# A macaron block on one core: the first tile, the two changes of stage and the last store put in another order

## The chip, the cores and the metric

The kernel runs on one core of one Trainium2 chip. The metric is the time of one execution on the device in microseconds (us); less is better. PE is TensorE, DVE VectorE, ACT ScalarE, POOL GpSimd, and SP the engine whose queue issues the DMAs.

## What is computed

x has 8 batches of 1024 rows of 128 numbers, all f32. Three residual steps follow one another, each on a layer norm of x:

```python
x = x + 0.5 * ffn(layernorm(x))
x = x + attn(layernorm(x))          # rotated q and k, causal softmax, one head of width 128
x = x + 0.5 * ffn(layernorm(x))     # the same weights

# ffn: 16 experts of width 64, 4 of them weighted per row, and one shared expert
scores = sigmoid(x @ gate_w.T)
w = scores of the 4 largest of (scores + gate_b), divided by their sum, times 2.5
y = sum_e w[e] * ((silu(x @ g_e.T) * (x @ u_e.T)) @ w2_e.T)  +  shared expert
```

## The kernel before

**Stages.** The first ffn runs over 16 tiles of 512 rows (T = 0 to 15), then attention over 8 batches, then the second ffn over 16 tiles (T = 16 to 31). All of x stays in SBUF, and the result is stored tile by tile in the second ffn. Every engine has its program written out by hand, with semaphores between them.

**One tile of the ffn.** All experts are computed, two at a time: `PAIRS` = 8 units of two experts, and unit 8 is the shared one (`UNITS` = 9). Each f32 product is made of three matmuls on a high and a low half of its factors (`mm3`). For a unit j, PE writes the gate and the up product to PSUM (`ffn_up`), ACT takes silu of the gate in place (`ffn_silu`), DVE multiplies by the row's weights of the two experts (`ffn_weighted`) and by the up product (`ffn_h`), ACT rounds this h to its high half (`ffn_h_hi`), POOL subtracts to get the low half (`low_half`, `h_lo_done`), and PE multiplies by w2 (`ffn_down`), three units later (`LAG`). After the last unit ACT copies the sum (`ffn_yT`), PE transposes it (`ffn_y`), and DVE adds it to x (`residual`).

**Routing.** During tile T the weights of tile T+1 are made: PE `ffn_logits`, then a chain of small DVE steps (`ffn_logit0` to `ffn_comb`, counted by `route_step`, 13 steps) with one ACT step in it (`ffn_gsilu`: score = silu(logit) / logit). PE transposes them (`ffn_combT`), ACT copies, and SP writes them to HBM and loads them back spread over the partitions (`comb_rows`, ten loads of up to 256 KB), which `ffn_weighted` reads.

**The first tile.** There is no time for that round trip, so for its first four units DVE copies the weights 64-fold into `spread`, PE transposes them (`comb_spread`), and ACT copies the result to `comb_s`. Only units 4 to 7 use the loads. The weights w13 come in two loads (`early`: 4 blocks, then 13) and are split by ACT and POOL. `warm` issues matmuls on zeros: 20, 5, 10 and 2 of them.

**From the first ffn to attention.** In tile 15 the projections of batch 0 (`qkv`), the rotation (`rope_cos` and `rope_add` on DVE, `rope_sin` on POOL) and the transposes (`qkT`) are woven in, by unit, by the tables `FIRST_STEPS`, `SIN_STEPS`, `COS_STEPS` and `ADD_STEPS`; ACT's copies come one unit later, at the end of the unit's work. After the tile PE does the first scores, `qkT` 2 and 3, the transposes of xn of batch 1 (`xnT` 0 and 1), and then `ffn_y(15)`.

**From attention to the second ffn.** In the last batch, `ffn_prep(i)` on each engine prepares tile 16 and the norm of tile 17 at row block i. Exp and Silu are in different tables of ACT.

## Time and profile before

| what | value |
|---|---|
| time, median of 3 runs | 886.3 us (885.8 to 886.94) |
| the profiled execution: its time | 890.32 us |
| its span in the profile | 888.5 us |
| PE busy | 866.8 us (98%) |
| DVE, ACT, POOL busy | 77%, 68%, 64% |
| mean granted clock of PE | 0.99 of full |

The span is from the first to the last instruction or transfer that the profile shows; 1.8 us lie around it. A view by stretches gives for each the busy time of the engines and the granted clock (1.00 is 2.4 GHz, 0.50 is 1.2 GHz). A line of the time line has start, duration, engine, line of the kernel, operation and tiles, and in brackets for how long the engine had been idle and who released it. A name of a tile can be that of the memory that it shares: `prob` stands for the weighted gate, `probT` for h, `cos` for `spread`, `sin` for `comb_s`, `qkv_both` for the loaded weights.

### The profile page before, as it was taken

The numbers are of one execution on the slowest core, as the hardware profiler recorded it, in microseconds if no ns is written. First come the engines' busy times: TensorE is split into PE (matmuls) and PEld (weight loads), VectorE is DVE, ScalarE is ACT, GpSimd is POOL, SyncE is SP. The second block draws the span as 40 slices with busy tenths as digits, with TensorE's granted clock in tenths as the row PEclk, the third lists the DMA queues.
The fourth block names the chain that finished last, engine by engine and source line by source line (L and its number), as shares of the span: only waits on it lengthen the run. The fifth ranks groups of instructions, "written<-read, shape, count | busy, mean of one in ns | idle before, by whom it ended". The sixth has DMA issues, their size and how long they took to land.

```text
span 888.5 us, 18704 instructions
## 1 busy us (share of the span) xinstructions
PE 866.8 (98%) x4634; PEld 732.4 (82%) x4634; DVE 687.3 (77%) x2123; ACT 603.3 (68%) x1255; POOL 568.3 (64%) x605
## 2 busy tenths in 40 slices
PE   8999999999999997999999999999999999999997
PEld 7778888888888875999999998788888888888885
DVE  6888888888888887565555656688888888888884
ACT  4666666666666675677777777776666666666664
POOL 5666666666667674866668763166666666666664
PEclk9999999999999999899999999999999999999998
DMA  3486444555554430000000000334455554444552
GB/s 119 134 236 144 108 108 109 122 132 134 136 122 96 97 97 1 1 1 1 1 0 0 0 0 0 97 97 110 120 132 137 132 124 108 108 109 122 137 133 63
DMA packets 58212, 80.61 MB, mean 91 GB/s; under 512 B 6464, under 2 KB 25152, under 8 KB 57920
## 3 DMA queue, kind: packets, MB, share of 16 engines
q1 hardware_dynamic: 58176, 80.19, 36.6%
q8 instruction: 15, 0.25, 0.1%
q14 instruction: 21, 0.17, 0.1%
HBM read 74.92 MB, written 5.24 MB: 90 GB/s over the span
## 4 chain that ended last, share of the span: by engine, by line
PE 56%; ACT 3%; DVE 2%; issue 1%; POOL 0%; ACTq 0%; DVEq 0%
PE bank L1189 49%; PE bank L1441 3%; PE bank L1405 2%; PE bank L1257 1%; PE bank L1236 1%; PE bank L1394 1%; ACT prob L651 1%; DVE xl L1069 1%; ACT probT L492 0%; ACT qkv_both L492 0%; ACT xh L492 0%; DVE probT L838 0%; ACT h_h L492 0%; DVE prob L829 0%; PE bank L1250 0%
## 5 line engine op out<-in xcount | busy, mean ns | idle before, releaser
L370 POOL TENSOR_TENSOR h_l<-probT,h_h 128x512 fp32r<-128x512 f32 x256 | 330.9, 1293 | 215.6 <-ACT h_h L492 215.4
L492 ACT ACTIVATE h_h<-probT 128x512 fp32r<-128x512 f32 (+1 forms) x288 | 180.2, 626 | 72.2 <-DVE probT L838 70.8
L1189 PE MATMUL bank<-xh,w_h 128*128 128x512 f32 x544 | 223.2, 410 | 0.3
L521 ACT ACTIVATE bank<-bank 128x512 f32<-128x512 f32 x256 | 148.6, 581 | 103.7 <-PE bank L1189 99.6
L1189 PE MATMUL bank<-xh,w_l 128*128 128x512 f32 x544 | 214.2, 394 | 0.0
L829 DVE TENSOR_TENSOR prob<-bank,qkT 128x512 f32<-128x512 f32 x252 | 173.6, 689 | 52.3 <-ACT bank L521 38.6
L1189 PE MATMUL bank<-xl,w_h 128*128 128x512 f32 x544 | 212.7, 391 | 0.0
L838 DVE TENSOR_TENSOR probT<-prob,bank 128x512 f32<-128x512 f32 x256 | 174.5, 681 | 11.5 <-DVE biased L772 5.0
L1189 PEld LDWEIGHTS bank<-xh,w_h 128*128 128x128 f32 x544 | 102.4, 188 | 23.4 <-DVE probT L838 3.5
L1189 PEld LDWEIGHTS bank<-xh,w_l 128*128 128x128 f32 x544 | 102.1, 188 | 23.7
L1189 PEld LDWEIGHTS bank<-xl,w_h 128*128 128x128 f32 x544 | 102.6, 189 | 19.2
L1189 PE MATMUL bank<-h_h,w_h 128*128 128x512 f32 x288 | 116.9, 406 | 1.5 <-POOL h_l L370 1.1
L1189 PE MATMUL bank<-h_h,w_l 128*128 128x512 f32 x288 | 113.6, 395 | 0.0
L1189 PE MATMUL bank<-h_l,w_h 128*128 128x512 f32 x256 | 101.3, 396 | 0.0
L492 ACT ACTIVATE probT<-bank 128x512 f32<-128x512 f32 (+2 forms) x128 | 64.8, 515 | 49.4 <-PE bank L1441 46.8
L1189 PE MATMUL bank<-qkv_both,probT 128*128 128x128 f32 x576 | 76.0, 277 | 2.4 <-ACT probT L492 1.3
L1189 PEld LDWEIGHTS bank<-qkv_both,probT 128*128 128x128 f32 x576 | 71.7, 192 | 4.8 <-issue 1.8
L466 POOL TENSOR_TENSOR rope_c<-qkv_both,cos 128x256 f32<-128x256 f32 x56 | 41.0, 733 | 48.2 <-ACT qkv_both L492 48.2
L499 ACT ACTIVATE xn<-X,neg_shift,rstd 128x128 f32 (+1 forms) x128 | 61.2, 485 | 9.9 <-POOL neg_shift L379 9.9
L1189 PEld LDWEIGHTS bank<-h_h,w_h 128*128 128x128 f32 x288 | 54.2, 188 | 15.0 <-POOL h_l L370 1.8
L1189 PE MATMUL bank<-qkT 128*128 128x512 f32 (+3 forms) x288 | 65.7, 355 | 0.0
L1189 PEld LDWEIGHTS bank<-h_h,w_l 128*128 128x128 f32 x288 | 54.2, 188 | 10.8
(103 smaller groups left out, 1396.2 us busy)
## 6 DMA issues: line engine op xcount, KB each, us to landing
...
```

Of the source, the lines that this page charges most:

```text
L370: nc.gpsimd.tensor_tensor(lo, f, hi.bitcast(F32), ALU.subtract).then_inc(done, 1)
L466: nc.gpsimd.tensor_tensor(rope_c[s][:], qkv[p][:, n, 0:2 * D].rearrange("p (w d) -> p w d", w=2), cos[:, n, :, :], ALU.mult).then_inc(rope ...
L492: return nc.scalar.activation(dst, src, ACT.Copy)
L499: ins = nc.scalar.activation(xn[:, n, :], X[:, bass.ds(NB * Tx + n, 1), :].rearrange("p a d -> p (a d)"), ACT.Identity, bias=neg_shift[:, ...
L521: nc.scalar.activation(bank[:, G_BANK[g], :], bank[:, G_BANK[g], :], ACT.Silu).then_inc(silu_done, 1)
L651: nc.scalar.activation(prob[s][:, 0:w], bank[:, 2 * s:2 * s + 2, :].rearrange("p a c -> p (a c)")[:, 0:w], ACT.Exp, bias=negmax[s][:], sca ...
L829: nc.vector.tensor_tensor(weighted[j % 2], bank[:, G_BANK[(q + j) % 2], :], comb_s[:, j, :] if spread_out else comb_b[q][:, j, :], ALU.mul ...
L838: nc.vector.tensor_tensor(h[g], weighted[j % 2], bank[:, U_BANK[j % 2], :], ALU.mult).then_inc(h_done, 1)
L1069: nc.vector.tensor_tensor(xl_half[n][:], bank[:, m, :], xh_half[n][:].bitcast(F32), ALU.subtract).then_inc(a_xl_done, 1)
L1189: return nc.tensor.matmul(dst, lhsT, rhs, start=start, stop=stop)
L1405: ins = nc.tensor.transpose(bank[:, m, c:c + P], rot[(2 * n + a) % ROPE_BUFS][:, w, :], ident[:])
L1441: ins = nc.tensor.transpose(bank[:, probT_bank(i, c, last), a * P:(a + 1) * P], prob[s][:, k0:k0 + P], ident[:])
```

## The change

It touches four places.

- **First tile.** w13 comes in three loads (4, 4 and 9 blocks). The silu of units 0 to 3 goes to SBUF (`silu_s`), and the spread weights are read where PE put them, in PSUM. The spread of units 0 and 1 is made by four DVE operations straight from `wsel` and `rsum`, before `ffn_comb`, that of 2 and 3 by two ACT copies. PE runs four gate and three up products ahead of the spread, then two more gates and two ups, with three banks for up (`START_U_BANK`). `ffn_xl(0, 0)` goes ahead of the statistics of tile 1. `warm` issues 16 and 5.
- **From the first ffn to attention.** ACT makes its copies for attention at the head of a unit. POOL makes the shift of batch 1 behind its last low half of the tile, and `rope_sin` and `rope_cos` of blocks 6 and 7 come earlier. ACT asks for its Exp table on a dummy before the `qkT` 2 copy. PE does `ffn_y(15)` ahead of the xn transposes of batch 1, and DVE `residual` ahead of `qkT` 3.
- **From attention to the second ffn.** The score of tile 16 is 1 / (1 + exp(-logit)), by Exp. ACT normalizes tile 17 at i = 6 instead of i = 7, ahead of its copies of the last `probT`, and asks for the Silu table at i = 7.
- **End.** In tile 31 DVE makes the low halves of units 7 and 8, PE orders its last products by what is there first, and copy, transposes, residual and store go in two halves.

Semaphores, tensors and calls that only follow from these are left out below, and some indentation. Constants:

```diff
-SPREAD_BANK = 4, 6
+SPREAD_BANK = 4, 5, 4, 4
...
-SIN_STEPS = [[], [0], [], [1], [2], [3], [4], [5], [6]]
-COS_STEPS = [[], [0], [], [1, 2], [], [3, 4], [], [5], [6]]
...
+      ("qkT", 0): 5, ("qkv", 5): 7, ("qkv", 6): 5, ("qkT", 1): 7, ("qkv", 7): 5, ("qkT", 2): 5, ("qkT", 3): 7}
+SIN_STEPS = [[], [0], [], [1], [2], [3], [4], [5, 6], [7]]
+COS_STEPS = [[], [0], [], [1, 2], [], [3, 4], [], [5, 6], []]
...
+ON_DVE = 2
+AHEAD = 3
+WARM = 16, 5
...
-early = slice(0, 2 * EARLY), slice(2 * EARLY, 2 * UNITS - 1)
+early = slice(0, 4), slice(4, 8), slice(8, 2 * UNITS - 1)
```
SP:

```diff
+load(w13_f[:, early[1], :], w13T[:, early[1], :], w13_loaded[1])
 load(X[:, NB:2 * NB, :], x_v[:, NB:2 * NB, :], x_loaded[1])
-load(w13_f[:, early[1], :], w13T[:, early[1], :], w13_loaded[1])
+load(w13_f[:, early[2], :], w13T[:, early[2], :], w13_loaded[2])
 load(w2_f, w2T, w2_loaded)
...
-        store(TILES - 1)
+        for a in range(2):
+            sp.wait_ge(x_done, 2 * TILES + a)
+            sp.dma_start(out_v[:, end_blocks(a), :], X[:, end_blocks(a), :]).then_inc(stored, 16)
```
POOL (the first piece is in the loop over units):

```diff
+        if last and first_batch is None and j >= PAIRS - 1:
...
-                pool.wait_ge(a_neg_shift_done, 2)
-            elif first_batch == 1:
-                pool.wait_ge(rope_s_done, QB - 1)
+            if first_batch == 1:
+                pool.wait_ge(rope_s_done, QB)
...
-        elif j == PAIRS - 1 and first_batch == 0:
+        elif j == PAIRS and first_batch == 0:
+            pool.wait_ge(h_lo_done, UNITS * (T + 1))
...
         low_half(w13_l[:, early[0], :], w13_f[:, early[0], :], w13_h[:, early[0], :], w13_split[0])
+        pool.wait_ge(w13_hi[1], 1)
+        low_half(w13_l[:, early[1], :], w13_f[:, early[1], :], w13_h[:, early[1], :], w13_split[1])
         pool.wait_ge(neg_shift_done, 1)
...
         ffn_tile(TILES - 1, 1, True, 1)
-        pool.wait_ge(h_lo_done, UNITS * TILES)
-        rope_sin(0, 0, QB - 1)
```
ACT:

```diff
-    if j < PAIRS:
+    if isinstance(T, int) and T == 0 and j < SPREAD:
+        nc.scalar.activation(silu_s[:, j, :], bank[:, G_BANK[g], :], ACT.Silu).then_inc(silu_done, 1)
...
 def comb_spread(j):
-    act.wait_ge(spread_ready, j + 1)
-    copy(comb_s[:, j, :], bank[:, SPREAD_BANK[j % 2], :]).then_inc(spread_done, 1)
+    act.wait_ge(route_step, ROUTE)
+    copy(spread[:, j, :, :].rearrange("p n (a r) -> p n a r", a=2),
+         comb[:, 2 * j:2 * j + 2, :].rearrange("p a (n r) -> p n a r", r=1
+                                               ).to_broadcast([P, NB, 2, INTER])).then_inc(spread_copied, 1)
 def ffn_tile(T, Tx, q, first, last, first_batch=None, start=False):
     for j in range(UNITS):
+        if first_batch == 1 and j >= 1:
+            for item in FIRST_STEPS[j - 1]:
...
         if j == 0 and not last and not start:
             ffn_xh(T + 1, 1 - q)
         if j == (7 if start else 6) and not last:
             ffn_combT(T + 1, 1 - q)
-        if not start or j >= 1:
+        if not start or j >= SPREAD:
...
             for n in XN_STEPS[j]:
                 attn_xn(1, n)
-            for item in FIRST_STEPS[j - 1] if j else []:
...
         act.wait_ge(w13_loaded[1], 16)
         copy(w13_h[:, early[1], :], w13_f[:, early[1], :]).then_inc(w13_hi[1], 1)
+        ffn_xh(base, 0)
         ffn_gsilu(base)
+        ffn_silu(base, 0, 0)
+        act.wait_ge(w13_loaded[2], 16)
+        copy(w13_h[:, early[2], :], w13_f[:, early[2], :]).then_inc(w13_hi[2], 1)
+        ffn_silu(base, 0, 1)
+        ffn_silu(base, 0, 2)
         for n in range(NB):
             ffn_xn(base + 1, 1, n)
-        ffn_silu(base, 0, 0)
         act.wait_ge(w2_loaded, 16)
         copy(w2_h[:], w2_f).then_inc(w2_hi, 1)
-        comb_spread(0)
         ffn_combT(base, 0)
-        comb_spread(1)
+        comb_spread(2)
         ffn_xh(1, 1)
-        comb_spread(2)
+        ffn_silu(base, 0, 3)
+        ffn_h_hi(base, 0, 0)
         comb_spread(3)
     ffn_tile(base, 0, 0, True, False, None, start)
...
+    if start:
+        attn_item(("qkv", 7), 0, 0, True)
     ffn_h_hi(T, 1, UNITS - 1)
     if start:
-        attn_item(("qkv", 7), 0, 0, True)
+        nc.scalar.activation(table[:, 0:1], X[:, B * QB, 0:1], ACT.Exp)
         attn_item(("qkT", 2), 0, 0, True)
         attn_exp(0, 0, 0)
-    ffn_yT(T, 1)
+        ffn_yT(T, 1)
+    else:
+        ffn_end(T)
+def ffn_end(T):
+    act.wait_ge(down_done, UNITS * (T + 1))
+    act.wait_ge(y_ready, T)
+    for a in range(2):
+        cols = slice(2 * P * a, 2 * P * (a + 1))
+        copy(yT[:, cols], bank[:, Y_BANK[1], cols]).then_inc(yT_half, 1)
 def attn_item(item, b, p, prologue=False):
...
-        ffn_gsilu(T)
+        ffn_exp_neg(T)
     elif i == 6:
         ffn_combT(T, 0)
-    elif i == 7:
         for n in range(NB):
             ffn_xn(T + 1, 1, n)
+    elif i == 7:
+        nc.scalar.activation(table[:, 1:2], X[:, B * QB, 0:1], ACT.Silu)
```
DVE:

```diff
+def ffn_denominator(T):
+    dve.wait_ge(gsilu_done, T + 1)
+    nc.vector.tensor_scalar_add(logit[:], gsilu, 1.0).then_inc(route_step, 3)
+def ffn_sigmoid(T):
+    dve.wait_ge(route_step, ROUTE * T + 4)
+    nc.vector.reciprocal(score, logit[:]).then_inc(route_step, 1)
...
+    if isinstance(T, int) and T == 0 and j < SPREAD:
+        dve.wait_ge(spread_ready, j + 1)
+        nc.vector.tensor_tensor(weighted[j % 2], bank[:, SPREAD_BANK[j], :], silu_s[:, j, :],
+                                ALU.mult).then_inc(weighted_done, 1)
...
+        low_half(h_h[k][INTER:P, :], h[g][0:INTER, :], h_h[k][0:INTER, :], h_lo_end)
+def ffn_end(T):
+    for a in range(2):
+        dve.wait_ge(y_half, a + 1)
+        xt = X[:, end_blocks(a), :]
+        nc.vector.scalar_tensor_tensor(xt, bank[:, END_BANK[a], 0:2 * P].rearrange("p (n d) -> p n d", d=D), 0.5, xt,
+                                       ALU.mult, ALU.add).then_inc(x_done, 1)
...
     if start:
-        ffn_weighted(T, q, 0)
-        ffn_h(T, q, 0)
+        for j in range(2):
+            ffn_weighted(T, q, j)
+            ffn_h(T, q, j)
         ffn_xl(N, 1 - q)
         dve.wait_ge(x_loaded[2], 16)
         for n in range(NB):
             ffn_stats(L, Lx, n)
-        ffn_weighted(T, q, 1)
...
         ffn_stats_wait(L)
         ffn_mv(L)
...
+        ffn_h(T, q, 2)
         ffn_var(L)
         ffn_logit0(N)
-        ffn_weighted(T, q, 2)
         ffn_away0(N)
         ffn_logit(N)
-        ffn_h(T, q, 2)
+        ffn_weighted(T, q, 3)
         ffn_recip(N)
-        ffn_weighted(T, q, 3)
+        ffn_h(T, q, 3)
         ffn_score(N)
         ffn_bias(N)
         ffn_biased(N)
...
         if first_batch == 1:
             attn_start(PAIRS)
+        else:
+            ffn_h_lo(T, q, PAIRS - 1)
...
+    ffn_xl(0, 0)
     dve.wait_ge(x_loaded[1], 16)
...
-    ffn_xl(0, 0)
     ffn_logit0(0)
...
     ffn_top4(0)
-    ffn_weights(0)
+    ffn_wsel(0)
+    ffn_wsum(0)
+    ffn_rsum(0)
+    comb_spread(0)
+    comb_spread(1)
+    ffn_comb(0)
+def comb_spread(j):
+    dve.wait_ge(route_step, ROUTE - 1)
+    for a in range(2):
+        e = 2 * j + a
+        ins = nc.vector.scalar_tensor_tensor(spread[:, j, :, a * INTER:(a + 1) * INTER],
+                                             wsel[:, :, e:e + 1].to_broadcast([P, NB, INTER]), ROUTE_SCALE,
+                                             rsum[:].rearrange("p (n r) -> p n r", r=1).to_broadcast([P, NB, INTER]),
+                                             ALU.mult, ALU.mult)
+    ins.then_inc(spread_set, 1)
...
         ffn_start()
-        dve.wait_ge(route_step, ROUTE)
-        for j in range(SPREAD):
-            nc.vector.tensor_copy(spread[:, j, :, :].rearrange("p n (a r) -> p n a r", a=2),
...
     if start:
+        rope_add(0, QB - 2)
         rope_cos(0, 0, QB - 1)
-        rope_add(0, QB - 2)
+        rope_add(0, QB - 1)
         dve.wait_ge(scores_ready, 1)
         attn_max(0, 0)
-        rope_add(0, QB - 1)
         attn_item(("qkT", 2), 0, 0, True)
+        residual(base + TILES - 1, TILES - 1)
         attn_item(("qkT", 3), 0, 0, True)
-    residual(base + TILES - 1, TILES - 1)
+    else:
+        ffn_end(base + TILES - 1)
...
-        ffn_recip(T)
     elif i == 5:
-        ffn_score(T)
+        ffn_denominator(T)
+        ffn_sigmoid(T)
         ffn_bias(T)
```
PE:

```diff
-    if j >= 2:
-        pe.wait_ge(spread_done, j - 1)
-    pe.wait_ge(spread_set, j + 1)
+    if j < ON_DVE:
+        pe.wait_ge(spread_set, j + 1)
+    else:
+        pe.wait_ge(spread_copied, j - ON_DVE + 1)
+        pe.wait_ge(weighted_done, 1 if j == 2 else j)
     for n in range(NB):
-        ins = nc.tensor.transpose(bank[:, SPREAD_BANK[j % 2], n * P:(n + 1) * P], spread[:, j, n, :], ident[:])
+        ins = nc.tensor.transpose(bank[:, SPREAD_BANK[j], n * P:(n + 1) * P], spread[:, j, n, :], ident[:])
     ins.then_inc(spread_ready, 1)
+def start_gate(j):
+    if 2 <= j < SPREAD + 2:
+        pe.wait_ge(silu_done, j - 1)
+    elif j >= SPREAD + 2:
+        pe.wait_ge(weighted_done, j - 1)
+    mm3(bank[:, G_BANK[j % 2], :], w13_h[:, 2 * j, :], w13_l[:, 2 * j, :], xh[0][:], xl[0][:]).then_inc(gate_ready, 1)
+def start_u(j):
+    if j >= AHEAD:
+        pe.wait_ge(h_done, j - AHEAD + 1)
+    mm3(bank[:, START_U_BANK[j % 3], :], w13_h[:, 2 * j + 1, :], w13_l[:, 2 * j + 1, :],
+        xh[0][:], xl[0][:]).then_inc(up_ready, 1)
...
     pe.wait_ge(w13_split[0], 1)
-    for j in range(EARLY):
-        ffn_up(0, 0, j, None)
-    warm(WARM[2])
+    for j in range(AHEAD):
+        if j == 2:
+            pe.wait_ge(w13_split[1], 1)
+        start_gate(j)
+        start_u(j)
+    start_gate(AHEAD)
     comb_spread(0)
+    comb_spread(1)
     ffn_combT(0)
-    comb_spread(1)
-    warm(WARM[3])
     ffn_xnT(1)
     comb_spread(2)
+    start_u(3)
+    pe.wait_ge(w13_split[2], 1)
+    start_gate(4)
+    start_u(4)
+    start_gate(5)
+    ffn_logits(1, 1)
     comb_spread(3)
+    pe.wait_ge(w2_split, 1)
+    pe.wait_ge(weighted_done, 2)
+    ffn_down(0, 0, 0)
+    for j in range(5, UNITS):
+        if j >= 6:
+            start_gate(j)
+        if j < PAIRS:
+            start_u(j)
+        if j == 6:
+            ffn_combT(1)
+        ffn_down(0, 0, j - AHEAD - 1)
+    ffn_down(0, 0, UNITS - LAG - 1)
...
         attn_item(("qkT", 3), 0, 0, True)
+    ffn_y(T)
     if start:
-        for item in STEP_ITEMS[0][:2]:
-            attn_item(item, 1, 1)
...
+        attn_item(("xnT", 0), 1, 1)
+def ffn_end(T):
+    Y = bank[:, Y_BANK[1], :]
+    a, b = PAIRS - 1, PAIRS
+    pe.wait_ge(h_hi_done, UNITS * T + a + 1)
+    mm(Y, w2_h[:, a, :], h_h[a % 3][:], False, False)
+    mm(Y, w2_l[:, a, :], h_h[a % 3][:], False, False)
+    pe.wait_ge(h_hi_done, UNITS * T + b + 1)
+    mm(Y, w2_l[0:INTER, b, :], h_h[b % 3][0:INTER, :], False, False)
+    pe.wait_ge(h_lo_end, 1)
+    mm(Y, w2_h[:, a, :], h_l[a % 3][:], False, False)
+    pe.wait_ge(h_lo_end, 2)
+    mm(Y, w2_h[:, b, :], h_h[b % 3][:], False, True).then_inc(down_done, 2)
+    pe.wait_ge(x_done, T)
+    for n in range(NB):
+        c = n % 2
+        if c == 0:
+            pe.wait_ge(yT_half, n // 2 + 1)
+        ins = nc.tensor.transpose(bank[:, END_BANK[n // 2], c * P:(c + 1) * P], yT[:, n * P:(n + 1) * P], ident[:])
+        if c == 1:
+            ins.then_inc(y_half, 1)
...
             attn_scores(b, p, i + 1)
         elif not last:
             attn_scores(b + 1, 1 - p, 0)
-        before, after = ([], []) if last else ([], STEP_ITEMS[0][2:]) if first and i == 0 else step_items(i)
+        before, after = ([], []) if last else step_items(i)
```
## Rows read from the trace of the kernel before

**Rows 1.** The page: busy time and share of the engines, first line.

```profile
PE 866.8 (98%) x4634; PEld 732.4 (82%) x4634; DVE 687.3 (77%) x2123; ACT 603.3 (68%) x1255; POOL 568.3 (64%) x605
```

**Rows 2.** The chain that ended last: start us, us, what (second ffn).

```profile
597.14 1.38 PE bank L1189 x6
...
616.84 1.38 PE bank L1189 x6
```

**Rows 3.** Time line, first tile, all engines but SP, 8 to 39 us.

```profile
8.64 1.28 PE L1189 MATMUL bank<-X 128*128 128x128 f32 x10
...
11.37 0.30 DVE L750 TENSOR_REDUCE bank<-bank 128x64 f32<-128x128 f32 x1 [1.21 <-PE bank L1189]
...
11.54 1.60 ACT L492 ACTIVATE w_h<-qkv_both 128x1664 fp32r<-128x1664 f32 x1 [2.11 <-DMA qkv_both<-in_w13T]
...
13.21 6.58 POOL L370 TENSOR_TENSOR w_l<-qkv_both,w_h 128x1664 fp32r<-128x1664 f32 x2 [2.77 <-ACT w_h L492]
13.34 0.23 DVE L768 TENSOR_TENSOR bank<-bank,rlogit 128x64 f32<-128x64 f32 x1 [0.57 <-ACT bank L510]
...
15.98 0.28 DVE L816 SCALAR_TENSOR_TENSOR comb<-bank,rsum 128x64 f32<-128x64 f32 x1
16.29 4.46 DVE L1026 COPY cos<-comb 128x512 f32<-128x512 f32 x4
...
20.67 0.68 DVE L829 TENSOR_TENSOR prob<-bank,sin 128x512 f32<-128x512 f32 x1
...
23.59 0.69 DVE L743 TENSOR_TENSOR xl<-bank,xh 128x512 fp32r<-128x512 f32 x1 [1.52 <-ACT xh L492]
...
34.62 0.33 PE L1250 MATMUL bank<-ident,comb 128*128 128x128 f32 x1
...
38.98 0.60 PE L1236 MATMUL bank<-ident,xn 128*128 128x128 f32 x4
```

**Rows 4.** Line 1026, DVE's four copies: shortest, median and longest in ns.

```profile
L1026 DVE COPY cos<-comb x4: 415/706/2866, 16.3 to 20.3; 128x512 f32<-128x512 f32 x4
```

**Rows 5.** By stretches: PE, PEld, DVE, ACT, POOL busy, granted clock, DMA share, GB/s.

```profile
22.00:23.00 1.00, 1.00 (x7) 1.00 (x6) 0.07 (x1) 0.04 (x1) 0.00 (x0) 0.50 0.78 213
...
359.00:361.00 2.00, 2.00 (x8) 1.87 (x7) 0.32 (x2) 1.45 (x4) 1.59 (x3) 0.50 0.00 0
```

**Rows 6.** Time line, from tile 15 to batch 0, 343 to 356 us.

```profile
343.26 1.24 DVE L1052 TENSOR_TENSOR rope_c<-qkv_both,cos 128x256 f32<-128x256 f32 x1
...
347.47 1.28 ACT L651 ACT_TABLE_LOAD   x1
...
350.97 1.71 PE L1394 MATMUL bank<-ident,xn 128*128 128x128 f32 x8 [1.97 <-DVE qkT L1074]
...
355.35 0.66 PE L1189 MATMUL bank<-wqkv_h,xh 128*128 128x384 f32 x1 [0.56 <-DVE xl L1069]
```

**Rows 7.** Time line, last batch to tile 16, 559 to 570 us.

```profile
559.76 0.98 PE L1441 MATMUL bank<-ident,prob 128*128 128x128 f32 x7 [0.66 <-ACT prob L651]
...
564.32 2.02 PE L1189 MATMUL bank<-qkv_both,probT 128*128 128x128 f32 x16 [0.34 <-ACT probT L492]
564.54 1.64 ACT L499 ACTIVATE xn<-X,neg_shift,rstd 128x128 f32<-128x128 f32 x4
...
569.51 0.69 DVE L829 TENSOR_TENSOR prob<-bank,qkT 128x512 f32<-128x512 f32 x1 [0.48 <-ACT bank L521]
```

**Rows 8.** Time line, the end, from 879 us.

```profile
879.37 0.69 DVE L841 TENSOR_TENSOR probT<-prob,bank 64x512 f32<-64x512 f32 x1 [0.28 <-ACT prob L524]
...
882.53 0.50 PE L1189 MATMUL bank<-h_h,w_h 128*128 128x512 f32 x1 [0.39 <-POOL h_h L370]
...
883.30 0.60 ACT L492 ACTIVATE probT<-bank 128x512 f32<-128x512 f32 x1 [2.58 <-PE bank L1189]
...
885.11 0.69 DVE L865 SCALAR_TENSOR_TENSOR X<-bank,X 128x512 f32<-128x512 f32 x1 [5.05 <-PE bank L1257]
885.83 0.40 SPq L321 DMA_DIRECT2D out_x<-X  x1
```

103 lines of the change are left out of this document (56 added, 47 removed).

## The prediction

> **What bounds the kernel now.** I read the page first: PE is busy for 98% of the span [rows 1], so nothing is won by making another engine faster in the steady part. The chain that ended last says the same: in the second ffn the same piece of PE work comes back after 19.70 us for every tile (616.84 less 597.14), and nothing but PE stands between [rows 2]. What can be won lies where PE waits or does work that counts for nothing, and the change touches just the places where that happens. So I read the time line of each, and ask one question: by how much does PE come earlier to the first piece of work behind which it never waits again? What is won before such a point is kept to the end, since the loops behind it are PE's.
>
> **First tile.** PE starts tile 1 (xn transposes) at 38.98, behind the transpose of tile 1's weights at 34.62, which follows at once on DVE's `ffn_comb(1)` [rows 3]. DVE is what sets this tile. Its main work starts at 20.67, with `ffn_weighted(0)`. The reader is to see what stands ahead of it: four copies that take 4.46 us [rows 3].
>
> Step 1, the logits. Four of 20 fill matmuls go; a fill record takes 0.13 us (1.28 / 10), two records make one, so PE would be free up to 1.0 us earlier, but then waits for xn. Against this, the split of xn is now in front of the statistics, which delays the first step of the route (11.37). I take -0.4 (0 to -0.7).
>
> Step 2, the score. It starts at 13.34 after 0.57 of idling for ACT's silu, which stood behind the 1.60 us copy of the 13 weight blocks (from 11.54) [rows 3]. That copy now comes behind gsilu. So -0.5 more: the route is 0.9 earlier, and DVE is where `ffn_comb` began (15.98) at 15.1.
>
> Step 3, the spread. DVE now makes four operations of 256 elements for the first two units. No row has one of this form. The nearest below is `ffn_comb` itself, 64 elements, 0.28; above, a DVE operation of 512 elements, 0.69 [rows 3]. Between, with their overlap, I take 0.37 each: 1.5 in all (1.0 to 2.8). With `ffn_comb` that puts `ffn_weighted(0)` at 16.9, 3.8 before the 20.67 of now. PE's transposes of the first spread run under the second one.
>
> Why the copies took 4.46: of the four, the shortest took 0.415 us and the longest 2.87 [rows 4], while POOL ran its low halves, 6.58 us from 13.21 on [rows 3]. One copy sat until POOL was done. The Trainium skill, page "SBUF — State Buffer", section "SBUF: two separate sides", has the rule: DVE operations of certain kinds and GpSimd take a shared port pair as an exclusive lock, for the whole instruction. The long copy agrees. By it the new operations, with one input in PSUM and one in SBUF, wait for nobody, and my 1.5 stands. If they were held as the copy was, it would be the case "held" below.
>
> Step 4, the DVE work up to `ffn_comb(1)`. Now 20.67 to 34.6, 13.9 us. 1.52 of it is a wait for ACT's xh [rows 3]; it goes, since PE and ACT are now ahead with the transposes of tile 1. What is left, 12.4, is the same list of operations without a gap; I take 12.5 (12 to 13.5). So `ffn_comb(1)` ends at 29.4, 5.2 earlier.
>
> Step 5, PE. It has to be ready by then. It has 11 groups of three 512-column matmuls (0.69 each: six take 1.38 [rows 2]) done before unit 5, where it had 4. Behind the transpose of the weights it now has one `ffn_down` more, 0.7: tile 1 starts 4.5 earlier. PE idles about 2 us before that, where gate 6 waits for `ffn_weighted(4)`. The clock was 0.50 at 22 to 23 us, behind a PE that had waited between the spreads [rows 5]. Such a fall again costs 0 to 1.3; I take 0.3. ACT's spread copies, POOL's splits and the extra SP issue (0.40, as the one in [rows 8]) lie beside all this: ACT wants the second w13 load only after the first, and DVE wants the X load later than now, since the split of xn is in front of it. POOL's last split ends about 20, and its first low half is wanted by `ffn_h(2)` at 22. First tile: **-4.2** (-2.5 to -5.2).
>
> **Tile 15 to batch 0.** The end point is the first qkv product of batch 1 at 355.35, behind which the batch runs on PE [rows 6]. In tile 15 ACT's copies at the head of a unit take away some PE waits, but DVE sets the pace there and gives back most. What stays: the rotation `cos` of block 6 begins at 343.26, behind ACT's copy [rows 6]; now it is ahead of `ffn_h(8)`. That makes `qkT` 1 come 1.9 earlier, and the maximum of row block 0 1.4 earlier. The table load, 1.28, [rows 6] goes from between `qkT` 2 and exp to a place where ACT waits for PE anyway: exp 2.5 earlier, `ffn_yT` 2.3. Then `ffn_y(15)` no longer stands behind `qkT` 3, the wait of 1.97 and the eight xn transposes of 1.71 [rows 6]: the residual is 5 earlier. Behind it come now the low half of `qkT` 3 and the maximum, 1.1 together. Sum at the qkv product: **-4.7** (-3.0 to -7.2).
>
> The lower bound: DVE has now cos 5, cos 6 and the add of 4 before `ffn_h(8)`, and each cos can be 1.24 long. The upper bound is the clock. At 359 to 361 it is 0.50 with PE busy all the time [rows 5], after the 1.97 wait. If PE does not fall, work of some 5 us at half speed takes half: -2.5 more.
>
> On the table load page and trace differ. The row has 1.28 from the end of the copy before to exp's start, with 0.01 between. The Trainium skill, page "ScalarE: Activation LUTs", section "What ACT_TABLE_LOAD costs", gives 2.66 us for a switch, a drain of 1.38 included. By the page this term would be -6.1; the measurement decides.
>
> **Last batch to tile 16.** Two table loads go from ACT's path and PE loses its wait of 0.66 before the transposes at 559.76 [rows 7]. But the four normalizations, 1.64, which ran beside PE's product at 564.32 [rows 7], now stand in front of the copy that this product waits for. With 0.7 won before, the weights are copied at about 562.5, the normalizations end at 564.1 and the copy at 564.7: the product starts 0.4 later than now. What sets the end is `ffn_weighted` of tile 16 at 569.51, 0.48 after DVE was ready, since silu had its table load [rows 7]. That load is hidden now, so DVE starts when ready: 0.4 later and 0.5 earlier, **0.0** (-0.4 to +1.8, with a clock fall in the new wait of 1.6).
>
> **End.** PE's last group waits until 882.53 for POOL, and ACT's copy is at 883.30 [rows 8]. POOL's two low halves lie ahead of it one behind the other, 1.3 each. DVE takes 0.69 for one of 512 elements, has nothing else behind 879.37 + 0.69, and ACT's high halves come a little before each: both are made by 881.4, and one matmul is left: copy at 881.9, not 883.30. Half copies, transposes and residuals overlap: now 883.30 to 885.80, 2.5; in halves I take 1.85 (1.5 to 2.5): -0.65. A second store issue (0.40 [rows 8]) is under the second half. **-2.1** (-1.4 to -2.5).
>
> **Sum.** -4.2 - 4.7 + 0.0 - 2.1 = -11.0. The profiled execution took 890.32 (888.5 span and 1.8 around it): 879.3 by its own time. The median of the runs is 886.3, 4.0 lower, and no term scales with that: **875.3**.
>
> **Rivals.**
> - *PE keeps its clock at the start of batch 0*: 2.5 more, 872.8. For it: the gaps of about 2 us become several of at most 0.8. Against it: they are many, and PE is busy little more than half of the time there.
> - *Held or late*: the first tile gives little. If the new spread operations are held until POOL's 9-block split ends (16.4), 1.5 is lost; with the clock at half behind the 2 us wait of step 5, 1.0 more; or the new wait of the last batch takes 1.5: 878.3. The page's lock speaks against the first part, rows 5 for the second.
> - *It does not do what it says*: tile 1 has its own gate, `ffn_weighted(0)` of tile 1, which waits for the round trip of `comb_rows`, and the residual of tile 15 moves but not the products behind it. Only the end is left: 884.2. Against it: that trip starts with the transpose of the weights (34.62), 4 earlier too.
> - *Slower*: the fills that go (4 of 20, and all 12 behind the routing) held PE's clock up. One place: from 9 to 34 us. PE's real work there is 23 groups of 0.69 and about 3 us of transposes and logits, 19 us at full clock; at half all along it would take 19 more, 894. It decides from 11 us on. Against it: PE now has products where the fills were, and falls last a few us in the rows. [...]
>
> **How the numbers follow.** Forecast (873.8 to 877.2) 0.50, clock kept 0.18, held or late 0.25, not done 0.04, slower 0.02, none of these 0.01. The measurement tells apart about 0.2%, 1.8 us. Faster by more than that: 0.50 + 0.18 + 0.25 + 0.04 = 0.97, less 0.01 for sums of bad ends, 0.96; same 0.02; slower 0.02. The range takes in the first three with their own widths: 871.5 to 879.5.
>
> **What the profile after would show.** Step 2: score at about 12.4. Step 3: `ffn_weighted(0)` near 16.9, and no DVE operation longer than 0.5 before it. Step 5: tile 1's xn transposes at 34.5. Batch 0: Exp table load ahead of the `qkT` 2 copy, first qkv product of batch 1 about 8.9 earlier than 355.35. Tile 16: its first weighted operation unchanged against that shift. End: last matmul to last residual under 2 us. I am wrong if DVE has waits above 1 us between 17 and 29 us, if PE's clock is 0.50 for more than 4 us in the first tile, or if tiles in the loops take other than 19.70.

## The result and the profile after

Timed beside each other, the changed kernel takes 875.93 us (median of 4, 875.33 to 876.56) and the kernel before 886.62 us (median of 4, 885.8 to 887.35). The ratio is 0.988, with a 95% interval of 0.9863 to 0.9897: 10.7 us less. The profiled execution of the changed kernel has a span of 874.6 us; that of before had 888.5, so the two traces differ by 13.9, 3.2 more than the medians. A second profile of before, below, shows where most of the 3.2 come from.

The page's first line of engines, after (compare [rows 1]):

```profile
PE 858.0 (98%) x4602; PEld 725.2 (83%) x4602; DVE 684.9 (78%) x2124; ACT 601.5 (69%) x1255; POOL 566.0 (65%) x604
```

The chain that ended last, in the second ffn (start, us, what; compare [rows 2]):

```profile
592.75 0.44 PE bank L1355 x4
...
612.49 0.44 PE bank L1355 x4
```

PE is still all there is in a tile, but a tile takes 19.74 (612.49 less 592.75), not 19.70.

The time line of the first tile (compare [rows 3, 4]):

```profile
12.54 0.23 DVE L818 TENSOR_TENSOR bank<-bank,rlogit 128x64 f32<-128x64 f32 x1
...
15.19 1.42 DVE L1089 SCALAR_TENSOR_TENSOR cos<-bank,rsum 128x256 f32<-128x256 f32 x4
16.52 0.27 DVE L866 SCALAR_TENSOR_TENSOR comb<-bank,rsum 128x64 f32<-128x64 f32 x1
16.76 0.69 DVE L874 TENSOR_TENSOR prob<-bank,sin 128x512 f32<-128x512 f32 x1
...
27.12 0.54 PE L1271 MATMUL bank<-xh,w_h 128*128 128x512 f32 x1 [1.91 <-DVE prob L881]
...
28.89 0.28 DVE L866 SCALAR_TENSOR_TENSOR comb<-bank,rsum 128x64 f32<-128x64 f32 x1
...
35.15 0.60 PE L1355 MATMUL bank<-ident,xn 128*128 128x128 f32 x4
```

The four copies of 4.46 us have become four operations of 1.42 in all, and `ffn_weighted(0)` starts at 16.76, not 20.67. DVE has no wait from there to 31.8. PE's longest is the 1.91 us before gate 6, the gate product of unit 6; the next is 0.55. What comes of it stands in the view by stretches (PE, PEld, DVE, ACT, POOL busy, granted clock, DMA share, GB/s; compare [rows 5]):

```profile
27.00:28.00 1.00, 0.88 (x3) 0.74 (x4) 1.00 (x10) 0.00 (x0) 0.29 (x1) 0.72 1.09 376
28.00:29.00 1.00, 1.00 (x4) 0.81 (x3) 0.90 (x5) 0.72 (x2) 0.01 (x1) 0.50 1.00 371
...
352.00:354.00 2.00, 2.00 (x16) 1.87 (x15) 1.00 (x5) 1.45 (x4) 1.87 (x4) 1.00 0.00 0
```

The clock is at half (1.2 GHz) to about 31 us, 3.4 us in all. At the start of batch 0, where before it was at half, it stays full (1.00 in the last row). The time line there (compare [rows 6]):

```profile
338.81 1.28 ACT L656 ACT_TABLE_LOAD   x1
...
339.70 1.45 POOL L385 TENSOR_TENSOR h_h<-probT,h_h 64x512 fp32r<-64x512 f32 x1
339.94 1.49 DVE L1136 TENSOR_TENSOR rope_c<-qkv_both,cos 128x256 f32<-128x256 f32 x1
...
341.81 0.29 DVE L1165 CUSTOM_DVE_ANT_0 bank<-bank,mask 128x128 f32<-128x128 f32 x1
342.19 0.37 ACT L692 ACTIVATE prob<-bank,negmax 128x128 f32<-128x128 f32 x1 [1.11 <-DVE negmax L1165]
343.89 0.69 DVE L935 SCALAR_TENSOR_TENSOR X<-bank,X 128x512 f32<-128x512 f32 x1 [1.19 <-PE bank L1376]
...
346.26 0.41 PE L1271 MATMUL bank<-wqkv_h,xh 128*128 128x384 f32 x1 [0.38 <-DVE xl L1153]
```

The table is loaded while ACT has nothing else; the first qkv product of batch 1 starts at 346.26, not 355.35. The last batch (compare [rows 7]):

```profile
550.60 1.64 ACT L515 ACTIVATE xn<-X,neg_shift,rstd 128x128 f32<-128x128 f32 x4
552.14 1.06 ACT L508 ACTIVATE probT<-bank 128x512 f32<-128x512 f32 x2
...
552.87 2.02 PE L1271 MATMUL bank<-qkv_both,probT 128*128 128x128 f32 x16 [1.60 <-ACT probT L508]
...
557.49 0.69 DVE L881 TENSOR_TENSOR prob<-bank,qkT 128x512 f32<-128x512 f32 x1
```

The normalizations now stand in front of the copies, and PE waits 1.60. The end (compare [rows 8]):

```profile
868.28 0.68 DVE L763 TENSOR_TENSOR h_l<-probT,h_h 128x512 fp32r<-128x512 f32 x1
...
869.08 0.49 PE L1271 MATMUL bank<-h_h,w_l 64*128 64x512 f32 x1 [0.20 <-ACT h_h L508]
...
870.40 0.66 ACT L508 ACTIVATE probT<-bank 128x256 f32<-128x256 f32 x2 [1.37 <-PE bank L1271]
...
871.37 0.75 DVE L911 SCALAR_TENSOR_TENSOR X<-bank,X 128x256 f32<-128x256 f32 x2 [1.63 <-PE bank L1486]
871.83 0.91 SPq L365 DMA_DIRECT2D out_x<-X  x2
```

### The profile page after: what moved, and what is told of

Read it like the earlier page. It is cut to its first block, busy times and chain, and to the rows that moved or that the text cites. A ratio compares the mean times of both kernels' runs of the same rounds, so it can differ in the third digit from the quotient of the medians.

```text
span 874.6 us, 18644 instructions
## 1 busy us (share of the span) xinstructions
PE 858.0 (98%) x4602; PEld 725.2 (83%) x4602; DVE 684.9 (78%) x2124; ACT 601.5 (69%) x1255; POOL 566.0 (65%) x604
## 4 chain that ended last, share of the span: by engine, by line
PE 55%; DVE 3%; ACT 2%; issue 1%; POOL 0%; ACTq 0%; DVEq 0%
PE bank L1271 48%; PE bank L1580 3%; PE bank L1544 1%; PE bank L1376 1%; PE bank L1355 1%; DVE xl L1153 1%; PE bank L1533 0%; ACT xh L508 0%; ACT qkv_both L508 0%; ACT prob L692 0%; ACT xn L515 0%; ACT probT L508 0%; DVE prob L881 0%; DVE rope_c L1136 0%; PE bank L1369 0%
## 5 line engine op out<-in xcount | busy, mean ns | idle before, releaser
L543 ACT ACTIVATE bank<-bank 128x512 f32<-128x512 f32 x252 | 146.3, 581 | 103.4 <-PE bank L1271 98.9
```

The source lines that it names most:

```text
L543: nc.scalar.activation(bank[:, G_BANK[g], :], bank[:, G_BANK[g], :], ACT.Silu).then_inc(silu_done, 1)
```

## The experiments

The changed kernel was timed twice: medians of 875.93 and 876.32. Not every experiment had it beside it, but each had the kernel before, whose medians there were 886.0 to 887.7. So a difference of two medians from different chips is good to about 1 us. The positions in the profiles, counted from one event to another of the same execution, are finer. The diffs show the main pieces of an edit; what only follows from them is left out.

**Both kernels profiled again.** No edit. They answer for the 3.2 us between traces and medians.

> The kernel before, profiled a second time. Theory: its first profile (span 888.5, 4 us over the unprofiled median) was a bad draw, with the clock at half behind the 1.97 us wait at batch 0; a second has the first qkv product of batch 1 at 355.3 again but may lack the fall behind it, and a span nearer 885.5. Rival: the fall recurs and the span is 888 again; then profiling itself costs this kernel 2 to 3 us.

> The changed kernel once more, so that the next ones have it beside them on the same chip. 875.9 us expected. In its profile: the granted clock behind PE's 1.9 us wait before gate 6 of the first tile is either at half for some 3 us, as in the first profile, or stays full; then tile 1's xn transposes start 1.0 us earlier, at 34.1 to 34.2.

The kernel before took 887.44 us with a span of 885.6; the changed one 876.32 (875.33 to 876.41) with a span of 874.6. So the spans now differ by 11.0, like the times. Of before, second profile, the time line and the stretches at batch 0:

```profile
349.90 1.49 PE L1394 MATMUL bank<-ident,xn 128*128 128x128 f32 x8 [1.98 <-DVE qkT L1074]
...
354.06 0.66 PE L1189 MATMUL bank<-wqkv_h,xh 128*128 128x384 f32 x1 [0.56 <-DVE xl L1069]
```

```profile
350.00:352.00 2.00, 2.00 (x12) 1.84 (x12) 0.00 (x0) 0.60 (x1) 0.00 (x0) 0.61 0.00 0
352.00:354.00 2.00, 0.72 (x3) 0.18 (x1) 1.63 (x4) 0.46 (x2) 0.00 (x0) 0.50 0.00 0
354.00:356.00 2.00, 1.94 (x6) 1.97 (x7) 0.69 (x1) 1.25 (x4) 0.00 (x0) 0.50 0.00 0
356.00:358.00 2.00, 2.00 (x11) 2.00 (x10) 1.65 (x8) 0.55 (x2) 1.73 (x3) 0.68 0.00 0
```

The fall recurs behind the same wait, but lasts to 357, not to 361. The rival that profiling itself costs 2 to 3 us falls: 887.44 lies among the 884.43 to 889.25 of the seven executions beside it. The first profile was a bad draw, and the longer fall is only a part of it. Its span is 2.9 longer. Of this, 0.4 is there at tile 1's start, 0.6 comes in tile 1, 0.2 up to the first qkv product of batch 1, 1.1 behind it through the longer fall, 0.1 from there to tile 31's last silu, and 0.5 behind that. The 0.6 in tile 1 is not the clock, which stays at 1.00: DVE waits there for the load of the weights, and PE's work behind it comes late. The time line of before, first profile:

```profile
47.33 0.69 DVE L829 TENSOR_TENSOR prob<-bank,qkT 128x512 f32<-128x512 f32 x1 [0.80 <-DMA qkT<-comb_rows]
```

In the second profile this wait is gone. Of the changed kernel, the fall behind gate 6 recurs too: tile 1 starts at 35.20, again not at 34.2.

With the second profile of before, the gain adds up like this (before, after, us):

| point | before | after | shift | of the part ahead of it |
|---|---|---|---|---|
| xn transposes in tile 1 | 38.55 | 35.15 | -3.40 | first tile -3.40 |
| the same, eleven tiles on | 255.32 | 252.29 | -3.03 | tiles +0.37 |
| first qkv product of batch 1 | 354.06 | 346.26 | -7.80 | tile 15, batch 0 -4.77 |
| row block 5's transposes, last batch | 553.20 | 543.73 | -9.47 | batches -1.67 |
| tile 16's first weighted operation | 567.14 | 557.49 | -9.65 | last batch -0.18 |
| tile 31's last silu | 876.25 | 866.98 | -9.27 | tiles +0.38 |
| end of the span | 885.6 | 874.6 | -11.00 | end -1.73 |

The end of the second profile of before, copy and last residual:

```profile
880.88 0.60 ACT L492 ACTIVATE probT<-bank 128x512 f32<-128x512 f32 x1 [2.58 <-PE bank L1189]
...
882.22 0.69 DVE L865 SCALAR_TENSOR_TENSOR X<-bank,X 128x512 f32<-128x512 f32 x1 [4.58 <-PE bank L1257]
```

**First tile undone.** The first tile as in the kernel before; the rest as changed.

```diff
-                comb_spread(0)
-                comb_spread(1)
-                ffn_comb(0)
+                ffn_weights(0)
...
+                    for j in range(SPREAD):
+                        nc.vector.tensor_copy(spread[:, j, :, :].rearrange("p n (a r) -> p n a r", a=2),
...
+                copy(comb_s[:, j, :], bank[:, SPREAD_BANK[j % 2], :]).then_inc(spread_done, 1)
```

> The changed kernel with the first tile as before (spread of the weights by DVE copies of comb and ACT copies out of PSUM, 20 fill matmuls and the later ones, two w13 loads), everything else as changed. Theory: the first-tile term stands by itself, so this is 3.8 to 4.5 us slower than the changed kernel (about 880.1), which is what the two traces show at tile 1's xn transposes (38.98 against 35.15) and one tile later (59.31 against 54.89). Rival: what is won at the start is partly lost later because tile 15's work or the loads meet PE at another moment: then less than 3 us.

880.14 us (877.9 to 881.29, 6 runs): 3.8 to 4.2 over the two medians of the changed kernel, as expected. But the profile does not put all of it in the first tile. Tile 1 starts at 38.49, 3.3 later than 35.15, and another 0.7 comes at the start of batch 0, where this profile has a fall that the changed kernel's own never had:

```profile
345.00:346.00 1.00, 1.00 (x5) 0.90 (x4) 0.98 (x4) 0.53 (x3) 0.00 (x0) 0.50 0.00 0
```

So the first tile and the clock are mixed in the 3.8 to 4.2. The table of all executions, below, parts them.

**Tile 15 and batch 0 undone.**

```diff
-                    nc.scalar.activation(table[:, 0:1], X[:, B * QB, 0:1], ACT.Exp)
...
                     attn_item(("qkT", 2), 0, 0, True)
-                    residual(base + TILES - 1, TILES - 1)
                     attn_item(("qkT", 3), 0, 0, True)
+                    residual(base + TILES - 1, TILES - 1)
...
-                ffn_y(T)
                 if start:
-                    attn_item(("xnT", 0), 1, 1)
+                    for item in STEP_ITEMS[0][:2]:
+                        attn_item(item, 1, 1)
+                ffn_y(T)
```

> The changed kernel with tile 15 and the start of batch 0 in the order of before (qkT 2 and 3 banks, rope blocks 5 to 7, Exp table not fetched ahead, residual and y after qkT 3 and both xn transposes). Theory A (order alone): +4.7 to +5.3 us, 881, and the granted clock may stay 1.00. Theory B (order, and PE's clock falls behind the 2 us wait that comes back): +7.2 to +7.8 us, 883.5, with a clock of 0.50 in rows some 10 us behind tile 15's last product. The profile of this run decides between them.

880.67 us (879.79 to 881.7, 5 runs): 4.4 to 4.7 over the changed kernel. Time line and stretches of this run:

```profile
345.93 1.55 PE L1534 MATMUL bank<-ident,xn 128*128 128x128 f32 x8 [1.98 <-DVE qkT L1158]
```

```profile
348.00:350.00 2.00, 0.81 (x3) 0.18 (x1) 1.62 (x4) 0.36 (x2) 0.00 (x0) 0.50 0.00 0
350.00:352.00 2.00, 1.84 (x6) 1.87 (x7) 0.70 (x2) 1.34 (x4) 0.00 (x0) 0.50 0.00 0
```

The wait of 1.98 is back, and the clock falls behind it, as theory B says; but the time is nearer to theory A's 881. Counted from tile 1's start (34.12 here, 35.15 changed) the profiles show the maximum of row block 0 1.8 earlier in the changed kernel, exp 2.6, the residual 5.5, the product 4.9 (350.16 here), and 1.4 more between the product and tile 17's xn transposes (560.03 less 350.16, against 554.72 less 346.26). So the fall costs 1.4 here behind the product, and B's 2.5, taken from the longest fall, was too much. The whole is 6.3 by these two profiles and 4.4 to 4.7 by the medians. 1.0 of the difference is the first tile, which had no fall in this profile. The rest is the draw: this profile is of the slowest of the five executions, 1.0 over their median.

**Only the early table undone.**

```diff
-                    nc.scalar.activation(table[:, 0:1], X[:, B * QB, 0:1], ACT.Exp)
```

> The changed kernel without the early fetch of the Exp table behind tile 15; the table is loaded where exp needs it. The prediction counted the 1.28 us load as one of the parts of -4.7, so by it this is up to 1.3 us slower (877.5). Rival, from the trace of the changed kernel: exp of row block 0 waits for DVE's maximum (342.2), the copy of qkT 2 ends at 341.1, so the load would end at 342.4 and costs 0.2: within 0.3 us of the changed kernel. If a switch took 2.66 us, as page "ScalarE: Activation LUTs" of the Trainium skill has it, exp would come at 343.8, 1.6 late.

876.76 us (876.61 to 876.88, 4 runs), 0.4 to 0.8 over the changed kernel. Its time line:

```profile
340.83 1.28 ACT L691 ACT_TABLE_LOAD   x1
342.12 0.37 ACT L691 ACTIVATE prob<-bank,negmax 128x128 f32<-128x128 f32 x1
```

Tile 1 started at 34.90, so exp is 307.22 behind it against 307.04 (342.19 less 35.15): 0.2 late, as the rival said. This profile also has the clock at half between 341 and 345, which it never had in the changed kernel's own; with it the first qkv product comes 0.8 late against tile 1. The three unprofiled executions need no such fall: their mean clock is 0.998, that of the profiled one 0.995, and they take 876.61 to 876.78, beside 876.31 to 876.56 for the changed kernel's five executions at 0.998. That fits a load worth 0.2 as well as one worth 0.4, but not the 1.3. The load itself is 1.28 again, with 0.02 ahead of it and 0.01 behind. The Trainium skill, page "ScalarE: Activation LUTs", section "What ACT_TABLE_LOAD costs", has 2.66 for a switch with its drain, which would have put exp at 343.5. The trace does not agree, and the measurement decides.

**Last batch undone.** Score by Silu; tile 17's normalizations behind the copies of the last `probT`.

```diff
                 elif i == 4:
-                    ffn_exp_neg(T)
+                    ffn_gsilu(T)
                 elif i == 6:
                     ffn_combT(T, 0)
+                elif i == 7:
                     for n in range(NB):
                         ffn_xn(T + 1, 1, n)
-                elif i == 7:
-                    nc.scalar.activation(table[:, 1:2], X[:, B * QB, 0:1], ACT.Silu)
```

> The changed kernel with the score of tile 16 by Silu as before and xn of tile 17 behind the copies of probT(7). Theory (this part is worth about 0, gain of two table loads eaten by PE's 1.6 us wait for probT(7)): within 0.5 us of the changed kernel, 875.9. Rival 1: the part gave something, +0.7 to +1.8. Rival 2: the part costs, and undoing it gains 0.5 or more.

875.92 us (875.33 to 876.43, 4 runs): the same. As a whole the part is worth nothing that these runs can show.

**Only the normalizations moved back.**

```diff
                     ffn_combT(T, 0)
+                elif i == 7:
                     for n in range(NB):
                         ffn_xn(T + 1, 1, n)
-                elif i == 7:
                     nc.scalar.activation(table[:, 1:2], X[:, B * QB, 0:1], ACT.Silu)
```

> The changed kernel with tile 17's four normalizations behind the copies of probT(7), Silu table fetched after them. Theory: PE's 1.60 us wait before the product of row block 7 goes to about 0.3, but tile 17's xh then waits for the table load, so tile 16's first weighted operation comes 0.6 earlier (0.4 to 0.8) and the time is 875.3. Rival: that operation is set by other work and nothing changes.

875.41 us (874.76 to 875.96, 4 runs), beside 876.32 of the changed kernel on the same chip; the ranges overlap. The time line:

```profile
551.71 2.02 PE L1271 MATMUL bank<-qkv_both,probT 128*128 128x128 f32 x16 [0.34 <-ACT probT L508]
...
553.59 1.28 ACT L724 ACT_TABLE_LOAD   x1
...
557.11 0.69 DVE L881 TENSOR_TENSOR prob<-bank,qkT 128x512 f32<-128x512 f32 x1
```

PE's wait is 0.34 instead of 1.60, and the weighted operation comes 304.70 behind the tile transposes at 252.41, against 305.20: 0.5 earlier. Nearly the 0.6 expected. This profile has the clock fall in the first tile too, as the changed kernel's two have.

**End undone.**

```diff
-                    else:
-                        ffn_h_lo(T, q, PAIRS - 1)
-                        ffn_h_lo(T, q, PAIRS)
...
-                if not start:
-                    ffn_down(T, 1, UNITS - LAG)
-                    ffn_end(T)
-                    return
```

> The changed kernel with the end as before: POOL's low halves of units 7 and 8, one copy of y, one residual, one store. Theory: +2.0 to +2.1 us (878.0), as the traces have it from tile 31's silu(8) to the end (9.1 us before 7.1 after). Rival: the median gain is smaller than the traces show, since the sum of spans (13.9) is larger than the sum of medians (10.7): +1 or less.

877.3 us (877.03 to 878.0, 4 runs), 1.0 to 1.4 over the changed kernel: less than expected. By the profiles, counted from tile 1's start, it is 1.8 (875.4 less 34.17, against 874.6 less 35.15), nearly the 2.0. Its first tile, by the time line, is the other draw:

```profile
27.03 0.50 PE L1262 MATMUL bank<-xh,w_h 128*128 128x512 f32 x1 [1.90 <-DVE prob L875]
...
34.17 0.60 PE L1346 MATMUL bank<-ident,xn 128*128 128x128 f32 x4
```

The same wait, and the clock stays full: tile 1 starts 1.0 earlier than at 35.15. Of the eight profiles with this first tile's PE order and no fills, five show the fall (tile 1 at 34.82 to 35.27) and three do not (34.12, 34.17, and 34.62 with the DVE copies below).

**Fills before gate 6.** `fill` makes matmuls of zeros, as `warm` does, into the bank that held the last spread.

```diff
                 for j in range(5, UNITS):
+                    if j == 6:
+                        fill(14)
                     if j >= 6:
                         start_gate(j)
```

> The changed kernel with 14 fill matmuls (0.13 us each by the records of the start) in PE's wait before gate 6 of the first tile. Theory: the clock stays full in every execution, tile 1's xn transposes at 34.2 in the profile, and the median falls by 0 to 1.0 us, by how often the clock fell without them. Rival: the fills themselves delay gate 6, or the clock falls all the same; then 0 or slower.

875.7 us, and all four executions between 875.57 and 875.76; the changed kernel's eight lie at 875.3 to 875.5 (three) or at 876.3 to 876.6 (five), with its two profiled ones, both with the fall, among the upper. The time line:

```profile
24.95 3.29 PE L1271 MATMUL bank<-X 128*128 128x128 f32 x28
...
34.45 0.60 PE L1363 MATMUL bank<-ident,xn 128*128 128x128 f32 x4
```

The fills take 3.04 (gate 6 is at 27.99), 1.7 times what was reckoned (14 of 0.13), since a fill matmul has two records; they hold gate 6 back by 1.0, of which 0.3 arrives at tile 1. The clock stays full. One profile without a fall proves little, since three of eight had none without fills; the four equal times say more. That the changed kernel's two heights are fall and no fall is looked at again below.

**The first spreads by DVE copies.**

```diff
-                comb_spread(0)
-                comb_spread(1)
                 ffn_comb(0)
+                comb_spread(0)
+                comb_spread(1)
...
-                    ins = nc.vector.scalar_tensor_tensor(spread[:, j, :, a * INTER:(a + 1) * INTER],
...
+                nc.vector.tensor_copy(spread[:, j, :, :].rearrange("p n (a r) -> p n a r", a=2),
```

> The changed kernel with the first two spreads made by two DVE copies of 512 elements from comb in SBUF to SBUF, behind comb, as the kernel before did, in place of the four operations that read wsel from PSUM. Theory (a copy from SBUF to SBUF is held while POOL works on its low half): comb at 15.1 to 15.4, the first copy is held until POOL's split ends at 16.3, so it takes 1.0 us or more, and the first weighted operation comes at 17.1, 0.4 later than 16.65. Rival (not held, 0.42 each as the shortest of before): that operation comes at 16.3, 0.3 earlier, and the PSUM form of the spread was no gain.

875.87 us (875.84 to 877.04, 4 runs), the same as the changed kernel by the medians. The line of the copies (shortest, median and longest in ns), then the time line:

```profile
L1087 DVE COPY cos<-comb x2: 415/814/1214, 15.5 to 16.6; 128x512 f32<-128x512 f32 x2
```

```profile
13.73 2.69 POOL L385 TENSOR_TENSOR w_l<-qkv_both,w_h 128x1152 fp32r<-128x1152 f32 x1 [1.02 <-ACT w_h L508]
...
17.52 0.69 DVE L874 TENSOR_TENSOR prob<-bank,sin 128x512 f32<-128x512 f32 x1 [0.48 <-PE bank L1289]
```

The first copy is held until POOL is done (1.21 against 0.42), the theory's case. It ends at 16.70, 0.28 behind POOL's split. The weighted operation is 0.76 later than 16.76, 0.48 of it a wait for PE's transposes, which the four small operations had let start earlier. The profile had no clock fall, and tile 1 started at 34.62, 0.45 behind the 34.17 of the changed form without a fall. The medians hide this, since they mix executions with and without a fall. Like with like it is there: three executions took 875.84 to 875.89 at a mean clock of 0.999 or more, and the changed kernel's three at such a clock 875.33 to 875.48, so the four operations from PSUM give 0.4 to 0.6.

**Two versions meant to be faster.** Both have fills before gate 6 (9 and 4), the Silu table directly behind the last exp, and the normalizations behind the copies. The second also has another order of the first tile, on DVE as shown; ACT copies tile 1's weights right behind the silu of unit 6, and PE transposes them one unit later:

```diff
                     ffn_h(T, q, 3)
+                    ffn_weighted(T, q, 4)
                     ffn_score(N)
+                    ffn_h(T, q, 4)
...
                     ffn_taken(N)
-                    ffn_weighted(T, q, 4)
+                    ffn_weighted(T, q, 5)
                     ffn_mark(N)
-                    ffn_h(T, q, 4)
                     ffn_weights(N)
+                    ffn_h(T, q, 5)
```

> The changed kernel with 9 fill matmuls before gate 6 (0.217 us each by the run with 14, whose fills held gate 6 back by 1.0), the Silu table fetched directly behind the last exp, and tile 17's normalizations behind the copies of probT(7). Theory: no clock fall in the first tile, tile 1's xn transposes at 34.2 in every execution, tile 16's first weighted operation 0.9 earlier against its batch than in the changed kernel; median 874.4 (874.0 to 874.9), executions within 0.4 of each other. Rival: only one of the two parts holds, 875.2.

> The kernel with both edits (4 fills, since the wait is shorter) and the first tile's DVE order changed: weighted and h of unit 4 around the score, weighted of unit 5 before the marking; ACT copies tile 1's weights right behind silu 6. Theory (DVE order sets the first tile, not its amount of work): gate 6 at 26.0, tile 1's xn transposes at 33.0, 1.1 earlier than with a full clock now; median 873.3. Rival 1: tile 1's first weighted operation waits for its comb_rows, 5.5 us behind the copy of the weights, and the gain is given back there: 874.4. Rival 2: POOL's low half of unit 5 becomes late, gain 0.5.

The first took 875.11 us (874.72 to 875.29, 4 runs; 874.4 expected), the second 874.46 (874.0 to 875.08, 4 runs; 873.3 expected; ratio to before 0.9872, 0.9855 to 0.9888), with before at 886.0 on that chip. In the first, tile 1 starts at 34.10 as expected, but tile 16's weighted operation is only 0.6 earlier, not 0.9: the table load now delays the copy of the weights and of `probT`. The time line of the second:

```profile
25.11 0.69 DVE L883 TENSOR_TENSOR prob<-bank,qkT 128x512 f32<-128x512 f32 x1
...
33.18 0.60 PE L1367 MATMUL bank<-ident,xn 128*128 128x128 f32 x4
```

Tile 1 starts 0.9 earlier than in the first; 1.1 was expected. Its time is that of rival 1 (874.4), but not for rival 1's reason: the lead is still there at tile 16's weighted operation (554.88 against 555.85). Most of the 1.2 that are missing were missing in the first version already. All its four executions are below the eight of the changed kernel (875.33 and up), though the two were not timed beside each other. It is the fastest version of this study, 1.5 to 1.9 us under the change.

**Every execution beside its mean clock.** No edit. Each execution was recorded with the mean granted clock of its span, the unprofiled ones too. Here the times (us) are parted by it:

| version | mean clock 0.999 to 1.0 | 0.998 or less |
|---|---|---|
| changed, both times | 875.33, 875.33, 875.48 | 876.31 to 876.56 (five) |
| first tile undone | 877.9, 878.36 | 880.0 to 881.29 (four) |
| tile 15 and batch 0 undone | 879.79 | 880.51 to 881.7 (four) |
| last batch undone | 875.33, 875.62 | 876.22, 876.43 |
| normalizations back | 874.76, 875.02 | 875.79, 875.96 |
| end undone | 877.03 | 877.19 to 878.0 (three) |
| early table undone | none | 876.61 to 876.88 (four) |
| DVE copies | 875.84, 875.85, 875.89 | 877.04 |
| fills before gate 6, 14 | 875.57, 875.7, 875.76 | 875.7 |
| first faster version, 9 fills | 874.72, 875.2, 875.29 | 875.01 |
| second, 4 fills, other order | 874.0 to 875.08 (four) | none |

One fall of 3.4 us is 0.002 of such a mean. The mean also counts the stretch behind the last matmul, where the clock is at half in every profile and nothing is lost, so a value of 0.998 alone is no proof of a fall. Still, without fills no execution of the right column is as fast as one of the left column of the same version, and the changed kernel's right column lies 0.8 to 1.2 over its left, about what the fall in the first tile cost in the profiles. The versions with fills have no such gap. This bears out, for the unprofiled executions too, that the two heights are fall and no fall.

It also parts the terms. With a clock near full on both sides, undoing the first tile costs 2.4 to 3.0 and not 3.8 to 4.2. The old first tile has a fall of its own at 20 to 24 us in all three of its profiles, so some 1 us of the term goes through the clock. Undoing tile 15 and batch 0 costs 4.3 to 4.5 even so, by its one such execution: that term is order. Undoing the end costs 1.6 to 1.7, near the 1.8 of the profiles.

## Why the prediction was right, and what was wrong in it

The time was forecast at 875.3 and is 875.93; the sum of -11.0 is the difference of the second pair of spans, to the first decimal. The places and the order of size of the terms were right. That the sum fits so well is luck: one gain that the forecast left out pays for a first tile and an end that gave less, and for tiles that take longer. The measured median is not the time of a typical execution either, but lies between two heights, 875.4 and 876.4.

*First tile*: forecast -4.2, measured -3.4 against the second profile of before (-3.8 against the first, from which it was reckoned), undone 3.8 to 4.2. Steps 1 to 4 hold: logits at 11.01 (-0.36 against -0.4), score 12.54 (12.4 forecast), the spread 1.42 (1.5), `ffn_weighted(0)` 16.76 (16.9), `ffn_comb(1)` ends at 29.17 (29.4), no DVE wait up to there. The sign "no DVE operation longer than 0.5 before it" was put too wide: between the logits and 16.76 the reciprocal takes 0.55, as it did before, and none is longer. The term that was mis-sized is in step 5: the clock fall behind the 2 us wait, taken at 0.3, cost 0.7 to 1.1 where it came (34.82 to 35.27 against 34.12 and 34.17), in five profiles of eight. The 2 us of waiting were forecast, and so was the range of 0 to 1.3; the value belonged at its middle or upper part. It also slipped out of one place: 34.5 for tile 1 is 38.98 less 4.5 and leaves the 0.3 out, so by the forecast's own sum it should be 34.8. The fall lasted 3.4 us, under the 4 that I named as a sign of being wrong.

*Held or not, in step 3*: a DVE copy from SBUF to SBUF was held beside POOL's split (1.21 against 0.42), the operations with one input in PSUM were not (0.41 each beside the same split). The Trainium skill, page "SBUF — State Buffer", section "SBUF: two separate sides", has this as its rule: DVE in such a copy and GpSimd shut each other out for a whole instruction. The trace agrees: the copy is held, the operations with a PSUM input are not. The rival "held or late" fails in its first part and in its third, since the wait of 1.60 in the last batch came but cost nothing in the sum; its second, the clock at half behind the 2 us wait for 1.0, came true in five profiles of eight. The rivals "it does not do what it says" (884.2) and "slower" (894) are refuted by the time and by tile 1 at 35.15.

*Tiles*: forecast 19.70, measured 19.74 in every version with three or four parts of the change. This costs 0.75 over the 26 tiles of the table. It meets one of my conditions for being wrong, in a small way. Laid side by side, the rows of one tile drift apart by 0.02 to 0.03 us at the transposes and the first products behind them; why stays open, and no run tries it.

*Tile 15 to batch 0*: forecast -4.7, measured -4.77, undone 4.4 to 4.7. The steps inside hold too: maximum 1.8 earlier (1.4 forecast), exp 2.6 (2.5), residual 5.5 (5). Wrong was how I divided exp's 2.5, of which the load was to bring the 1.28. By the profiles the new order without the early load brings 2.4 of the 2.6, and the early load on top of it 0.2: the `qkT` 2 copy ends early enough (340.8) for a load behind it to be over by 342.1, and the maximum is there at 341.9. In the old order the early load could bring at most 0.8, since the maximum ends at 342.90 and exp starts at 343.72; no run has it alone. The two edits cover the same wait, and the order covers nearly all of it.

*PE keeps its clock at batch 0*: this was a rival at 0.18, 2.5 us and 872.8. Its mechanism came true: no fall there in nine of ten profiles of the changed order, a fall in three of three of the order before. Its time did not: it gave -1.67 against the second profile of before, and the other terms fell short by as much. I set its chance too low because I compared how busy PE was and not the longest wait: 1.98 before, 0.75 now. That the longest wait is what counts is argued, since the two orders differ in more than that, and two of eleven profiles fell behind waits of 0.64 and 0.75 all the same.

*Last batch*: forecast 0.0, measured -0.18, undone 0.0. The product at 564.32 comes 0.4 late against its batch (552.87, a shift of -11.45 where the batch has -11.83), and the new wait is 1.60, both as forecast.

*End*: forecast -2.1, measured -1.73, undone 1.8 by the profiles and 1.0 to 1.4 by the medians. Copy after the last silu: 4.63 before, 3.42 now, a gain of 1.2 for 1.4, since the product with unit 8's high half waits for ACT until 869.08. And the 2.5 us from copy to last residual that I read in [rows 8] was itself a draw with a slow clock: the second profile of before has 2.0 (880.88 to 882.91), so the halves save 0.3 and not 0.65.

So the sum was right because the clock kept at batch 0 (-1.7, not in the forecast) paid for the first tile (about 0.8), the tiles (0.75) and the end (0.4). For the time, the medians are the better base than the profiled execution: the first profile of before, with a fall to 361 us, a wait for a load in tile 1 and a slow end, made the traces differ by 13.9.
